# A decoder layer on one core: row loads issued by SP, four buffers for the sums of paired blocks, and three steps reordered

## The reference

```python
x = x + self_attention(layernorm(x))            # 16 heads of 16, causal window of 64
x = x + cross_attention(layernorm(x), ctx_1024) # 16 heads, relative bias by bucket, no window
x = x + experts(layernorm(x))
# experts: softmax router over 8, the best 2 kept and renormalised;
# y = sum_e p_e * ((silu(x @ gate_e + gb_e) * (x @ up_e + ub_e)) @ down_e + db_e)
```

## Time and profile before

| | us |
|---|---|
| median of 3 runs | 1213.61 |
| lowest, highest | 1212.24, 1214.14 |
| the profiled execution | 1211.85 |
| its span in the profile | 1210.2 |
| PE busy | 1168.2 (97%) |
| DVE, ACT, POOL busy | 868.3, 753.8, 821.0 |

### The profile page before, as it was taken

How to read it: one execution, slowest core, us unless ns; L and a number is a source line. 1 busy time by engine, 2 the same in 40 slices (tenths; PEclk the granted TensorE clock), 3 DMA queues, 4 the chain that set the end, 5 groups by cost and what they waited for, 6 DMA issues and landing times.

```text
span 1210.2 us, 36900 instructions
## 1 busy us (share of the span) xinstructions
PE 1168.2 (97%) x12874; PEld 1023.7 (85%) x12874; DVE 868.3 (72%) x3851; ACT 753.8 (62%) x1845; POOL 821.0 (68%) x1593
## 2 busy tenths in 40 slices
PE   6899999999999999999999999999899999999996
PEld 4688888888888888888888888887689999998995
DVE  3567888888888888888888888888777655544442
ACT  2567766767766767766766766766564555555552
POOL 4677788778788778788778788876636644444432
PEclk8999999999999999999999999999899999999998
DMA  8411122121122121112112112122765433333221
GB/s 191 93 43 47 50 59 75 50 58 58 51 58 75 50 58 58 51 59 75 52 58 59 51 58 71 48 65 87 230 212 140 76 57 54 53 58 56 46 32 23
DMA packets 70936, 86.11 MB, mean 71 GB/s; under 512 B 25600, under 2 KB 57728, under 8 KB 70752
## 3 DMA queue, kind: packets, MB, share of 16 engines
q1 hardware_dynamic: 54768, 58.60, 16.7%
q0 software_dynamic: 15552, 25.05, 10.7%
q10 hardware_dynamic: 432, 0.10, 0.0%
HBM read 43.10 MB, written 20.95 MB: 53 GB/s over the span
## 4 chain that ended last, share of the span: by engine, by line
PE 90%; DVE 4%; issue 2%; POOL 2%; DMA 1%; ACT 0%; POOLq 0%; DVEq 0%
PE bank_S L901 10%; PE bank_Q L824 7%; PE bank_P L824 6%; PE bank_Q L916 5%; PE bank_S L815 5%; PE bank_S L866 5%; PE bank_B L737 4%; PE bank_A L737 4%; PE bank_B L837 4%; PE bank_A L837 3%; PE bank_A L804 3%; PE bank_P L763 3%; PE bank_B L804 3%; PE bank_Q L876 3%; PE bank_B L796 3%; PE bank_S L754 3%
## 5 line engine op out<-in xcount | busy, mean ns | idle before, releaser
L628 POOL TENSOR_SCALAR arena<-arena,mC 112x375 f32<-112x375 f32 x512 | 297.6, 594 | 26.4 <-DVE mC L1282 24.3
L1282 DVE CUSTOM_DVE_ANT_0 arena<-bank_S,arena 112x375 f32<-112x375 f32 x512 | 260.4, 543 | 56.9 <-PE bank_P L824 30.4
L634 POOL TENSOR_SCALAR arena<-arena 112x112 f32<-112x112 f32 x512 | 175.0, 356 | 85.3 <-DVE arena L1270 85.3
L654 POOL DMA_INDIRECT out<-y,xb x63 | 106.6, 1692 | 83.8 <-DVE y L1420 48.6
L824 PE MATMUL bank_Q<-ident,arena 112*126 112x112 f32 x858 | 131.9, 262 | 2.1 <-POOL arena L628 1.5
L1071 ACT ACTIVATE pTC<-bank_P 126x336 f32<-126x336 f32 x226 | 102.6, 454 | 40.6 <-PE bank_P L824 16.9
L1270 DVE CUSTOM_DVE_ANT_0 arena<-bank_S,arena 112x112 f32<-112x112 f32 x512 | 102.1, 270 | 14.6 <-PE bank_S L754 14.6
L1071 ACT ACTIVATE pTC<-bank_Q 126x336 f32<-126x336 f32 x222 | 101.3, 456 | 18.1 <-PE bank_Q L824 14.6
L824 PEld LDWEIGHTS bank_Q<-ident,arena 112*126 112x126 f32 x858 | 96.2, 141 | 15.4 <-issue 9.7
L824 PE MATMUL bank_P<-ident,arena 112*126 112x112 f32 x678 | 107.9, 268 | 1.3 <-ACT pTC L1071 0.8
L647 POOL DMA_DIRECT2D xb<-xs x63 | 44.1, 700 | 80.1 <-issue 76.6
(11 more groups left out here) (263 smaller groups left out, 3566.9 us busy)
## 6 DMA issues: line engine op xcount, KB each, us to landing
arena<-in_l_ctxT SPq DMA_DIRECT2D x32, 378.0 KB, 3.5
k<-k_low SPq DMA_DIRECT2D x64, 188.0 KB, 2.3
xb<-xs POOLq DMA_DIRECT2D x63, 129.0 KB
q<-q SPq DMA_DIRECT2D x64, 112.0 KB
arena<-in_L_ffn_gate_w SPq DMA_DIRECT2D x8, 512.0 KB
arena<-in_L_ffn_up_w SPq DMA_DIRECT2D x8, 512.0 KB
arena<-in_L_ffn_down_w SPq DMA_DIRECT2D x8, 512.0 KB
arena<-in_x SPq DMA_DIRECT2D x32, 112.0 KB, 2.0
```

Source lines behind the costliest of these rows:

```text
L628: pool.tensor_scalar(z[n % NZ][:, 0:T], z[n % NZ][:, 0:T], -1.0, mC[:, n:n + 1], ALU.mult, ALU.add).then_inc(s_u, 1)
L634: m = pool.tensor_scalar(sF[r][:, j, :], sF[r][:, j, :], -1.0, mF[:, r, j:j + 1], ALU.mult, ALU.add)
L654: pool.indirect_dma_start(out=out[:, :], out_offset=bass.IndirectOffsetOnAxis(ap=xb[x][:, D + 1:D + 2].bitcast(I32), axis=0), in_=y2[x % 2 ...
L1282: dve.tensor_tensor_reduce(out=z[n % NZ][:, 0:T], in0=bank[f"S{r}"][0:S, 0:T], in1=nbias[:, n, :], scale=1.0, scalar=3.0e38, op0=ALU.add, ...
```

## The change

Four things are changed.

1. **Row loads move from POOL to SP.** `load`, `load_pair`, `tables_ready` and `add_and_load` are gone from POOL, whose `add` step is now only the add. SP gets `load_rows` and `load_behind`: at `get:n` it loads block n, and at `add:j` with even j (each j from 42 on) blocks j+10 and j+11 (j+10), after the same waits as before. SP walks through the steps in order.
2. **Four buffers for the sums of pairs.** `rows_out` gives pair k `y2` if k is even or above 17, else the two `xbT` tiles, which are used otherwise only by single blocks. `weigh_rows` waits for the adds of the pair two behind in place of the last one (pairs 19 and 20 and single blocks as before), and ACT's first use of `xbT` waits for the adds of pair 17.
3. **`TAIL_ORDER`:** `pkg:0` to `pkg:3` stay at the head; `pkg:4` to `pkg:9` stand behind the `get` steps with `pkg:10` to `pkg:15`. The first table's pieces `blocks:0` to `blocks:4` stand one by one between earlier steps. `pv3 oc3` of the last batch stand ahead of `x3T:-1 x3Tc:-1`.
4. **`PERIOD`:** `sc@-2` stands behind `u8@1` in place of behind `rs1@5`, so POOL scatters a batch before it masks the keys of another.

```diff
-pkg:0 pkg:1 pkg:2 pkg:3 pkg:4 pkg:5 pkg:6 pkg:7 pkg:8 pkg:9 v0 ln3:-2 t14:-1 st:-2 rs3:-2 t13:-1 p8:-1 v0c
+pkg:0 pkg:1 pkg:2 pkg:3 v0 ln3:-2 t14:-1 st:-2 rs3:-2 t13:-1 blocks:0 p8:-1 v0c p11:-1 t12:-1 pv0:-1 t15:-1
...
+            rows_out = [[y2[h] if k % 2 == 0 or k > NP - 4 else xbT[h] for h in range(2)] for k in range(NP)]
...
+                    def load_rows(j):
+                        r = sp.value_load(blocks[0:1, 0, j:j + 1], min_val=0, max_val=E * R)
+                        sp.dma_start(xb[j % XB][:, :], xs[bass.ds(r, P), :]).then_inc(s_xb[j % XB], 16)
+
+                    def load_behind(j):
+
+                        if j:
+                            sp.wait_ge(s_add, 16 * (j - (j > NFULL)))
+                        for n in (j + XB - 2, j + XB - 1) if j < NFULL else (j + XB - 2,):
...
+                            if n < NBLK:
+                                load_rows(n)
...
+                        elif step == "get":
+                            if b == 0:
+                                sp.wait_ge(s_blocks, 1)
+                                buffers_free(sp)
...
+                            load_rows(b)
+                        elif step == "add" and b % 2 == 0:
+                            load_behind(b)
...
-                    def load(j, x):
-                        r = pool.value_load(blocks[0:1, 0, j:j + 1], min_val=0, max_val=E * R)
-                        pool.dma_start(xb[x][:, :], xs[bass.ds(r, P), :]).then_inc(s_xb[x], 16)
...
-                            in_=y2[x % 2][:, :], in_offset=None, compute_op=ALU.add).then_inc(s_add, 16)
...
+                            in_=rows_out[j][:, :], in_offset=None, compute_op=ALU.add).then_inc(s_add, 16)
...
-                            add_and_load(b)
+                            add(b, b % XB)
...
+                        if j == NFULL:
+                            act.wait_ge(s_add, 16 * 2 * (NP - 3))
...
-                        if j >= 2:
-                            dve.wait_ge(s_add, 16 * (j - j % 2 if j < NFULL else max(j - 1, NFULL)))
+                        if j >= NFULL:
+                            dve.wait_ge(s_add, 16 * max(j - 1, NFULL))
+                        elif j // 2 > NP - 3:
+                            dve.wait_ge(s_add, 16 * (j - j % 2))
+                        elif j >= 4:
+                            dve.wait_ge(s_add, 16 * (j - j % 2 - 2))
```

More of the change, by code:

```diff
@@ L89 @@
[L89 to L98, removed]
@@ L100 @@
+bu:20
 """
@@ L299, in decoder_layer @@
                   for w, n, m in (("gw", DC, F), ("uw", DC, F))}
+            rows_out = [[y2[h] if k % 2 == 0 or k > NP - 4 else xbT[h] for h in range(2)] for k in range(NP)]
+            rows_out = [t if len(t.shape) == 2 else t[:, :, :].rearrange("p c s -> p (c s)") for k in rows_out for t in k] + \
+                [y2[j % 2] for j in range(NFULL, NBLK)]
             gates = s1("gates", [P, FC, 2 * P])
@@ L583, in _ @@
                             load_package(sp, e, half)
+                        elif step == "get":
+                            if b == 0:
+                                sp.wait_ge(s_blocks, 1)
+                                buffers_free(sp)
+                                for q in range(2):
+                                    need(sp, s_sc[q], 32 * ((B1 + 1 - q) // 2))
+                                    need(sp, s_st[q], 16 * ((B1 + 1 - q) // 2))
+                            load_rows(b)
+                        elif step == "add" and b % 2 == 0:
+                            load_behind(b)
+                    for j in range(1 + max(b for step, b in steps if step == "add"), NBLK):
+                        if j >= NFULL or j % 2 == 0:
+                            load_behind(j)
                     sp.wait_ge(s_add, 16 * NBLK)
@@ L700, in _ @@
                             scatter(b)
[L701 to L704, removed]
-                                for q in range(2):
-                                    need(pool, s_sc[q], 32 * ((B1 + 1 - q) // 2))
-                                    need(pool, s_st[q], 16 * ((B1 + 1 - q) // 2))
-                            load(b, b)
                         elif step == "add":
-                            add_and_load(b)
+                            add(b, b % XB)
                         elif step == "pad":
@@ L718, in _ @@
                     for j in range(1 + max(b for step, b in steps if step == "add"), NBLK):
-                        add_and_load(j)
+                        add(j, j % XB)
                 @block.tensor
```

58 lines of the change are left out of this document (26 added, 32 removed).

## The result

The changed kernel takes 1235.27 us (median of 4 runs, 1234.24 to 1236.49) against 1213.88 for the kernel before (now over four runs, the fourth of them 1218.78): ratio 1.017, 95% interval 1.0139 to 1.0201, about 21 us slower. The profiled execution took 1234.24 us with a span of 1232.2, which is 22.0 more than the span of before. TensorE's busy time is nearly the same, 1170.2 us against 1168.2; the other 20 of the 22 us are idle time.

A forecast was written before the change was run, and what follows sets the result against it. TensorE, busy for 97% of the span, was taken as the bound. Stall +17.2, clock +2.9, turn -1.8 and buffers -1.2 gave +17.1 on 1211.85, so 1229.0, stated as a median of 1230.5 us; range 1218 to 1238.

The forecast's parts named there:

- The forecast case: Whole kernel: a TensorE stall of 12 to 24 us, giving 1225 to 1238 us; chance 71%.
- the one stall: Before pair 5's transposes: TensorE waits until 929.0 for rows of blocks 10 and 11, +17.2 us.
- First row load: SP, step 1: cannot be issued before the store of batch 30's rows ahead of it, done at 858.3.
- The 0 for the spread table: Block table's pieces on VectorE: some run up to 7 us earlier, net 0, bounds -1 and +1.
- Ten slots: SP, step 2: ten row loads at 1.0 us each, bounds 0.43 and 1.15; half 4 at 868.3.
- Eleven half steps: SP, step 3: package halves 4 to 15 take 55.2 us, bounds 49.4 and 59; half 15 at 923.5.
- The end: SP, step 4: half 15's instructions and store 1.4 us, two row loads 2.0, landing 2.1; rows there at 929.0.
- The clock: TensorE behind the long stall: some microseconds at half clock, +2.9 us, bounds 0 and 3.
- The turn: From pairs to single blocks: adds land early enough without two loads ahead on POOL, -1.8 us.
- Four buffers: Weighting of pairs 2 to 18 no longer waits for the last adds; stall of 916 goes, -1.2 us.
- Gains ahead of pair 5: TensorE waits saved before pair 5's transposes (1.29, 0.47, 0.49 us) only lengthen the stall; worth nothing at the end.
- Later loads suffer too: Rival, blocks 12 and on: if SP doesn't catch up, each of ten pairs adds a microsecond, above 1240; chance 5%.

The follow-up runs named there:

- experiment 1: Changed kernel with the loads of blocks 10 and 11 issued on SP right behind block 9, ahead of half 4: 1226.91 us, ratio 1.0086.
- experiment 3: Changed kernel with the loads of blocks 10 and 11 issued behind half 12 of the packages: 1226.4 us, ratio 1.0073.
- experiment 4: Changed kernel with the old `TAIL_ORDER`, halves 4 to 9 ahead of all row loads on SP: 1231.08 us, ratio 1.0115.
- experiment 5: Changed kernel with blocks 10 and 11 loaded behind block 9, and 12 to 17 in pairs behind halves 10, 12 and 14: 1208.99 us, ratio 0.9954.
- experiment 12: As experiment 11, but with the block table's pieces spread as in the changed kernel: 1210.04 us, ratio 0.9958.
- experiment 11: As experiment 8, but with the last value group (`pv3 oc3`) ahead of `x3T:-1 x3Tc:-1`: 1206.52 us, ratio 0.9925.
- experiment 6: Kernel before with only the four buffers for the sums of pairs added: 1216.18 us, ratio 1.0012.
- experiment 2: Changed kernel with all row loads back on POOL, buffers and both order tables as changed: 1216.18 us, ratio 1.0005.
- experiment 8: Changed kernel with row loads between packages, old `PERIOD`, and old `TAIL_ORDER` except halves 4 to 9 behind the row loads: 1208.04 us, ratio 0.9945.
- experiment 9: Kernel before with only the changed `PERIOD`: 1216.58 us, ratio 1.0005.
- experiment 10: As experiment 8, but with two buffers for the sums (`y2` alone, waits as before): 1207.97 us, ratio 0.9941.
- experiment 7: Kernel before with only the changed `TAIL_ORDER`, row loads on POOL: 1216.88 us, ratio 1.0019.

## Why the prediction was right, point by point

The forecast case held: 1230.5 predicted, 1235.27 measured, inside 1218 to 1238, slower as given with 0.88. (The sum of the prediction, 1229.0 + 1.8, is 1230.8 and not 1230.5, which changes nothing.)

**What bounds it, and the one stall: right.** TensorE stood before pair 5's transposes for rows issued by SP behind half 15. Experiments 1, 3 and 4 move the stall by moving loads alone, and 5 removes it.

**Its size was off,** 17.2 forecast, 22.63 measured; the rows landed 6.3 us later than in the sum, TensorE was ready 0.9 later. By steps:

1. *First row load.* Its slot was to begin at 858.3. The slot begins with a read of the row number in SBUF, at 860.9, and the DMA follows at 861.90:

```profile
L524 SPq TENSOR_LOAD <-blocks x63: 262/268/511, 860.9 to 1164.0; - x63
L524 SPq FUSED_REGOPS  x63: 152/152/177, 861.4 to 1164.3; - x63
```

   That is 2.6 late: 1.07 by this execution, 1.2 because VectorE's sum ended at 860.13 in place of 857.9 + 1.07, and some 0.4 between store and load, five semaphore waits, that the sum had left out. The piece of the table ahead of the sum had grown:

```profile
857.45 0.15 DVE L1381 TENSOR_SCALAR diff<-cum 1x8 f32<-1x8 f32 x1
...
858.38 1.18 DVE L1384 TENSOR_TENSOR nd<-nd,diff 1x8 f32<-1x8 f32 x1
859.59 0.18 DVE L1385 SCALAR_TENSOR_TENSOR blocks<-iota,tbl 1x34 int32<-1x34 f32 x1
859.71 0.42 DVE L1507 TENSOR_TENSOR x<-bank_B,x 112x256 f32<-112x256 f32 x1
```

   It takes 2.3 us (857.45 to 859.77), where it took 1.15 before; the last section says what it met. The 0 for the spread table was wrong: it stands in front of the stores, and so of the row loads, which begin 1.3 us later for it in experiment 12, and TensorE itself loses 1.2 us there ahead of pair 0. In the changed kernel the 1.2 us by which the sum is late are part of the long stall for rows.
2. *Ten slots* were taken at 1.0: from 860.9 to half 4 at 872.68 is 11.8 us, 1.8 more. From one row load to the next it is 1.21 and 1.48 us at first and then 1.10 each (the 10.74 of the row above are nine such steps and the last instruction of 0.34). So ten slots took 1.18 each, a little over the upper bound of 1.15, and the steady slot is next to POOL's price.
3. *Eleven half steps*, 55.2: 56.9 measured (872.68 to 929.57), within 49.4 to 59. The row loads' leaving POOL did not speed the packages up. By the Trainium skill's page DMA: Bandwidth & Descriptors (Anatomy of one DMA) they would have been 44, the prediction's estimate. This trace disagrees as that of before did, with no half step under 4.1 us. The page gives its fit for single DMAs issued by GpSimd; these are pairs of DMAs issued by SP, and each step holds the way from the landing to the next issue as well.
4. *The end*, 5.5: 5.8 measured, 929.57 to 935.34.

**The clock,** +2.9: pair 5 to pair 6 takes 12.18 us; in experiment 11 it takes 10.86, of which 0.98 is a stall that the changed kernel doesn't have there. So 12.18 - 9.88 = 2.3 us of half clock. Right in kind, 0.6 too high. The stretch from which the 2.9 were taken cost 2.3 too: pair 0 to pair 1 takes 7.36 us before, 5.06 in experiment 11 with the clock at 1.00.

**The turn,** -1.8: TensorE waits nowhere there, and it is 2.04 us shorter. Right. The last adds are done 0.5 us sooner behind TensorE's end, which had been put at nothing (10.21 us in place of 10.67; 10.0 to 10.3 in all runs with the loads on SP, 10.7 to 10.9 in the others).

**Four buffers,** -1.2: right in this trace by chance. The stall of 916 is gone where a long pause stands just ahead of it, here and in experiment 3; experiments 1, 5, 6 and 11 have four buffers, no such pause before pair 5, and keep it (1.0 to 1.1 us). The step failed in its cause: the row had "issue" as what ended the wait, not an add.

**Gains ahead of pair 5** were absorbed, as said. **`PERIOD`:** nothing, as said. **"Later loads suffer too":** not in this kernel, since after the long stall SP had time to catch up; but experiment 1 shows that this was the luck of a larger loss. Pair 6's loads were as late as pair 5's, and whoever mends only the first meets the second.

## What to carry to other kernels

An issuing engine that waits in program order is a queue: before a load is put on it, list what stands ahead, what each of those waits for, and when the data are needed, and do so for every load behind the obstacle, not for the first alone. The Trainium skill's page DMA: Bandwidth & Descriptors (Issuing engine by pattern) recommends Sync for simple loads; here that was right by 0.5% once the loads stood between the packages, and wrong by 1.7% when they stood behind them. When a long stall is found, ask what it hides, since removing it uncovers the next.

## What was not expected of the hardware

An instruction on 8 numbers is not always short: the one of L1384 takes 1.18 us in the changed kernel and, as the same instruction on other lines, in experiments 1, 2, 3, 5 and 12; it takes 0.15 before and in 4, 6 and 8 to 11. The traces show what it meets. POOL starts three TENSOR_SCALAR on `arena`, of 0.6 us each, the first within 0.01 us of its start, and VectorE's instruction ends within 0.02 us of the end of the second:

```profile
858.38 1.79 POOL L665 TENSOR_SCALAR arena<-arena,mC 112x375 f32<-112x375 f32 x3
```

In experiment 7 the same three start at 859.07, and there it is another of the small instructions, the one at 859.08, that takes 1.18 us, while this one takes 0.36. So the length goes with what POOL does at that moment, and moving the table's pieces moved them under it. No run tried this by itself.

A row load costs SP 1.10 us in the steady run of them, nearly POOL's 1.15: 0.27 for the read of the row number, 0.34 for the DMA instruction, the rest registers and the steps between. The SP versions of the loads are also steadier from run to run: experiments 5, 8, 10 and 11 spread over 2 to 5 us (6 runs each), 12 over 3 (11 runs), and 2, 6, 7 and 9 with loads on POOL over 5 to 11 (10 or 12 runs each). What makes the difference was not tried. In the profiled execution of 7 two pairs take 10.00 and 9.97 us in place of 9.65. Whether the clock fell in the stretch of short stalls near 868 also differed between kernels whose stalls are all of 0.4 to 2.3 us: from 868 to 872 it was 0.50 before and in 7, 1.00 in 6 and 11. What decides it stays open.
